# Feed-forward part of a vision layer: eight groups written out, down weights turned behind gate/up, down result scaled in PSUM, last store in two halves

## What is computed

```python
def _act_fake_quant(x, clip_factor):
    scale = jax.nn.sigmoid(clip_factor) * jnp.max(jnp.abs(x)) / QMAX
    return jnp.clip(_ste_round(x / scale), -QMAX - 1.0, QMAX) * scale
xq = _act_fake_quant(x, clip_x[0])          # x = layernorm(h)
gate = jnp.einsum('bsh,ih->bsi', xq, _weight_fake_quant(w_gate))
up = jnp.einsum('bsh,ih->bsi', xq, _weight_fake_quant(w_up))
h = _act_fake_quant(jax.nn.silu(gate) * up, clip_down[0])
return jnp.einsum('bsi,hi->bsh', h, _weight_fake_quant(w_down))
```

## Time and profile before

| | |
|---|---|
| median of 3 runs | 777.65 us (776.64 to 777.92) |
| profiled execution, its own time | 776.94 us |
| its span, first to last instruction | 775.1 us |
| busy share: PE, DVE, ACT, POOL | 89%, 83%, 75%, 68% |
| mean granted TensorE clock | 0.966 |
| feed-forward part within the span | 675.1 to 775.1 us |

### The profile page before, as it was taken

How to read it: one execution, slowest core, us unless ns; L and a number is a source line. 1 busy time by engine, 2 the same in 40 slices (tenths; PEclk the granted TensorE clock), 3 DMA queues, 4 the chain that set the end, 5 groups by cost and what they waited for, 6 DMA issues and landing times. The chain is left out here.

```text
span 775.1 us, 26199 instructions
## 1 busy us (share of the span) xinstructions
PE 686.7 (89%) x9862; PEld 536.8 (69%) x9862; DVE 645.5 (83%) x1396; ACT 582.4 (75%) x1278; POOL 523.8 (68%) x791
## 2 busy tenths in 40 slices
PE   0498899999999999999999999999999999378674
PEld 0277678777877777878877877788788777244363
DVE  4788876899889988989898889889886997769957
ACT  3567878778788678869777877788778886379593
POOL 3449965957686859877677888388848886521174
PEclk9979999999999999999999999999999999879878
DMA  8301000000010000101000000000000000000014
GB/s 236 100 29 33 17 18 4 32 18 19 1 34 22 15 3 32 34 2 33 18 18 3 18 18 12 25 24 32 19 3 22 20 21 21 1 1 0 1 40 129
DMA packets 14958, 21.91 MB, mean 28 GB/s; under 512 B 1972, under 2 KB 11446, under 8 KB 14840
## 3 DMA queue, kind: packets, MB, share of 16 engines
...
q10 hardware_dynamic: 436, 0.40, 0.2%
...
## 5 line engine op out<-in xcount | busy, mean ns | idle before, releaser
L904 POOL TENSOR_TENSOR k_bd<-kT,rmask 128x400 f32<-128x400 f32 x192 | 167.7, 901 | 7.4 <-PE ps_s L1357 4.3
L805 ACT COPY pT<-ps_w 25x400 f32<-25x400 f32 x192 | 94.6, 493 | 9.3 <-PE ps_w L1372 6.7
L1398 PE MATMUL ps_w<-oy_hi,o_hi 128*128 128x512 f32 x192 | 94.9, 494 | 0.0
L913 POOL TENSOR_TENSOR prob_hi<-prob_hi,rsum 128x800 f32<-128x800 f32 x48 | 74.8, 1558 | 13.4 <-DVE rsum L1150 13.3
L1133 DVE TENSOR_REDUCE nmax<-ps_s 128x16 f32<-128x400 f32 x96 | 72.4, 766 | 11.5 <-PE ps_s L1357 11.3
L785 ACT COPY v_bd<-ps_w 50x256 f32<-50x256 f32 x192 | 70.3, 366 | 13.3 <-PE ps_w L1332 10.9
L1398 PE MATMUL ps_w<-oy_hi,o_lo 128*128 128x512 f32 x192 | 76.3, 397 | 0.0
L1398 PE MATMUL ps_w<-oy_lo,o_hi 128*128 128x512 f32 x192 | 76.2, 397 | 0.0
L826 ACT ACTIVATE ps_w<-ps_w 128x256 f32<-128x256 f32 x96 | 35.7, 372 | 51.8 <-PE ps_w L1398 50.4
L918 POOL TENSOR_TENSOR ln<-ln,ln_eps 128x1 f32<-128x1 f32 x96 | 20.0, 208 | 75.2 <-ACT ps_w L826 74.8
L1357 PE MATMUL ps_s<-k_bd,qT 64*25 64x200 f32 (+1 forms) x3072 | 70.5, 291 | 0.0
...
## 6 DMA issues: line engine op xcount, KB each, us to landing
...
```

The source lines that it names most:

```text
L805: last = nc.scalar.copy(pT[ROWB * h:ROWB * h + LQ, s % 2, c::2, :, 0:LQ], ps_w[row:row + LQ, bank].rearrange("p (j t) -> p j t", j=4)[:, : ...
L904: last = nc.gpsimd.tensor_tensor(k_bd[:, v % KBD, c], kT[:, w % 2, c, 2 * p * L:(2 * p + 2) * L].unsqueeze(1).broadcast_to([P, HR, 2 * L]) ...
L913: nc.gpsimd.tensor_tensor(pr, pr, rsum[:, s % 2, e].unsqueeze(2).broadcast_to([P, H, WIDTH[e]]), ALU.mult).then_inc(prob_ready, 1)
L1398: mm = nc.tensor.matmul(G[:], ot[:, s % 2, c, 2 * (p % 2):2 * (p % 2) + 2].rearrange("p b t -> p (b t)"), wt[:, w, c], start=False, stop=( ...
```

## The change

1. All hardware loops of the feed-forward part become straight-line code with constant addresses.
2. Head: the shift is made from `-mean*rstd`, computed while PE turns the maximum, so that scale and shift come out of one instruction. Two memsets move from DVE to POOL. POOL casts only two pairs of group 0, DVE casts the other two. The cast of the down weights comes behind the casts of groups 0 and 1 on POOL.
3. The down weights are turned at the end of gate/up, into banks 3 and 0 of `ps_w`, and ACT copies them out in place of DVE.
4. Down: the product with step and `drow` is written back to the PSUM banks it was read from; the addition reads `hidden` and PSUM; `o_s` is gone. PE waits for `result_ready` (the addition) in place of `down_read`.
5. Group 7 is scaled, added and stored in two halves of two pairs; the first waits for the sixth of the last twelve matmuls (`half_filled`).

```diff
     id32 = sb(stack, "id32", [P, P])
     id16 = sb(stack, "id16", [P, P], BF16)
     stat3 = sb(stack, "stat3", [P, NPAIR, 4])
-    rstd3 = sb(stack, "rstd3", [P, NPAIR])
+    norm3 = sb(stack, "norm3", [P, 2, NPAIR])
+    rstd3 = norm3[:, 0]
...
-    o_s = sb(ffn, "o_s", [P, 2, PAIRS, D])
...
-            with sp.Fori(0, GROUPS) as g:
-                sp.wait_ge(result_ready, g + 1 + T)
+            pieces = [(g * PAIRS, PAIRS) for g in range(GROUPS - 1)] + [(NPAIR - PAIRS, PAIRS // 2), (NPAIR - PAIRS // 2, PAIRS // 2)]
+            for i, (n, pairs) in enumerate(pieces):
+                sp.wait_ge(result_ready, i + 1 + T)
                 for row, b in HALVES:
-                    sp.dma_start(out[bass.ds(g * GB, GB)].rearrange("(q two) t d -> two t q d", two=2)[b],
-                                 hidden[row:row + L, bass.ds(g * PAIRS, PAIRS), :]).then_inc(stored, 16)
-            sp.wait_ge(stored, 32 * GROUPS)
+                    sp.dma_start(out[2 * n:2 * (n + pairs)].rearrange("(q two) t d -> two t q d", two=2)[b],
...
@@ -1522,8 +1527,12 @@
                     if f == 3 and g < GROUPS - 1:
                         y_out(1, GROUPS - 1)
 
+            for k, bank in enumerate((3, 0)):
+                act.wait_ge(wd_turned, k + 1)
+                nc.scalar.copy(wdT[:, :, k * P:(k + 1) * P],
+                               ps_w[:, bank].bitcast(BF16)[:, 0:FC * P].rearrange("p (f t) -> p f t", f=FC)).then_inc(wd_ready, 1)
             act.wait_ge(hstep_chain, 4)
...
             pool.sem_inc(hq_ready, 2 * T)
             pool.sem_inc(yq_ready, T)
+            nc.gpsimd.memset(mx[:], 0.0).then_inc(f_zeroed, 1)
+            nc.gpsimd.memset(one_f[:], 1.0).then_inc(f_zeroed, 1)
             nc.gpsimd.memset(w_q[:, :, I:], 0.0).then_inc(f_zeroed, 1)
+
+            def y_cast(g, pairs=PAIRS):
+                pool.wait_ge(yint_ready, g + 1)
+                if g > 0:
+                    pool.wait_ge(yint3_ready, g + 1)
+                pool.wait_ge(yT_filled, g - 1 + T)
+                nc.gpsimd.tensor_copy(y_q[:, g % 2, :, 0:pairs].rearrange("p k q t -> p q k t"),
+                                      y_int[:, g % 2, 0:pairs].rearrange("p q (k t) -> p q k t", k=KC)).then_inc(yq_ready, 1)
+            y_cast(0, PAIRS // 2)
+            y_cast(1)
             pool.wait_ge(wint_ready, KC)
             nc.gpsimd.tensor_copy(w_q[:, :, 0:I], w_int[:]).then_inc(wq_ready, 1)
-            for g in range(GROUPS):
-                pool.wait_ge(yint_ready, g + 1)
-                pool.wait_ge(yint3_ready, g + 1)
-                pool.wait_ge(yT_filled, g - 1 + T)
-                nc.gpsimd.tensor_copy(y_q[:, g % 2].rearrange("p k q t -> p q k t"),
-                                      y_int[:, g % 2].rearrange("p q (k t) -> p q k t", k=KC)).then_inc(yq_ready, 1)
+            for g in range(2, GROUPS):
+                y_cast(g)
             nc.gpsimd.memset(h_q[:, :, :, :, L:], 0.0).then_inc(f_zeroed, 1)
             for g in range(GROUPS):
                 r = g % 2
...
             for row, _ in HALVES:
                 nc.vector.tensor_reduce(mx[row:row + L, 0:1], tok[row:row + L, 0], AX.X, ALU.max).then_inc(y_max, 1)
+            dve.sem_inc(acts_ready, T)
+            dve.sem_inc(result_ready, T)
+            nc.vector.scalar_tensor_tensor(norm3[:, 1], mean, -1.0, rstd, ALU.mult, ALU.mult).then_inc(dev_chain, 1)
             dve.wait_ge(max_turned, 1)
...
             dve.wait_ge(step_chain, 1)
             nc.vector.reciprocal(mx[:, 4:5], sg[:, 0, 0:1]).then_inc(step_chain, 1)
             dve.wait_ge(step_chain, 2)
-            nc.vector.tensor_scalar(tok[:, 2], rstd, mx[:, 4:5], None, ALU.mult).then_inc(y_ready, 1)
-            dve.wait_ge(y_ready, 1)
-            nc.vector.scalar_tensor_tensor(tok[:, 3], mean, -1.0, tok[:, 2], ALU.mult, ALU.mult).then_inc(y_ready, 1)
+            dve.wait_ge(dev_chain, 4)
+            nc.vector.tensor_scalar(tok[:, 2:4], norm3[:], mx[:, 4:5], None, ALU.mult).then_inc(y_ready, 1)
...
                 largest(g, FP - 1, g * FP + FP)
-            dve.wait_ge(y_ready, 2)
+            dve.wait_ge(y_ready, 1)
             y_ints3(0, 0, 2)
+            dve.wait_ge(yint3_ready, 1)
+            nc.vector.tensor_copy(y_q[:, 0, :, PAIRS // 2:].rearrange("p k q t -> p q k t"),
+                                  y_int[:, 0, PAIRS // 2:].rearrange("p q (k t) -> p q k t", k=KC)).then_inc(first_q, 1)
             y_ints3(1, 1)
-            for k in range(KC):
-                dve.wait_ge(wd_turned, k + 1)
-                nc.vector.tensor_copy(wdT[:, :, k * P:(k + 1) * P],
-                                      ps_s[:, 1, k].bitcast(BF16)[:, 0:FC * P].rearrange("p (f t) -> p f t", f=FC)).then_inc(wd_ready, 1)
-            with dve.Fori(0, GROUPS // 2 - 1) as g2:
+            for g2 in range(GROUPS // 2 - 1):
...
 
-            def scaled(g, r):
+            def scaled(g, r, first=0, pairs=PAIRS):
+                ps = down_ps(r)[:, first:first + pairs]
+                nc.vector.scalar_tensor_tensor(ps, ps, sg[:, 1, 0:1], drow[:].unsqueeze(1).broadcast_to([P, pairs, D]),
+                                               ALU.mult, ALU.mult).then_inc(down_scaled, 1)
+                dve.wait_ge(down_scaled, g + first // 2 + 1)
+                h = hidden[:, g * PAIRS + first:g * PAIRS + first + pairs, :]
+                nc.vector.tensor_tensor(h, h, ps, ALU.add).then_inc(result_ready, 1)
+            for g in range(GROUPS - 1):
                 dve.wait_ge(down_filled, g + 1 + T)
-                nc.vector.scalar_tensor_tensor(o_s[:, r], down_ps(r), sg[:, 1, 0:1], drow[:].unsqueeze(1).broadcast_to([P, PAIRS, D]),
-                                               ALU.mult, ALU.mult).then_inc(down_read, 1)
-                dve.wait_ge(down_read, g + 1 + T)
-                h = hidden[:, bass.ds(g * PAIRS, PAIRS), :]
-                nc.vector.tensor_tensor(h, h, o_s[:, r], ALU.add).then_inc(result_ready, 1)
-            with dve.Fori(0, GROUPS // 2) as g2:
-                for r in (0, 1):
-                    scaled(g2 * 2 + r, r)
+                scaled(g, g % 2)
+            dve.wait_ge(half_filled, 1)
+            scaled(GROUPS - 1, 1, 0, PAIRS // 2)
+            dve.wait_ge(down_filled, GROUPS + T)
+            scaled(GROUPS - 1, 1, PAIRS // 2, PAIRS // 2)
 
...
                 pe.wait_ge(yq_ready, g + 1 + T)
+                if g == 0:
+                    pe.wait_ge(first_q, 1)
                 need(pe, yT_ready, g)
                 for k in range(KC):
...
-                    if isinstance(g, int) or r == 0:
-                        pe.wait_ge(wd_ready, KC)
                 for k in range(KC):
...
                     mm.then_inc(up_filled, 1)
             find_max(0)
             pe.wait_ge(drow_filled, 2)
-            pe.wait_ge(wq_ready, 1)
-            pe.wait_ge(f_zeroed, 3)
-            for k in range(KC):
+
+            def turn_wd(k, bank):
+                pe.wait_ge(wq_ready, 1)
+                pe.wait_ge(f_zeroed, 3)
                 for f in range(FC):
-                    mm = nc.tensor.transpose(ps_s[:, 1, k].bitcast(BF16)[:, f * P:(f + 1) * P], w_q[:, k, f * P:(f + 1) * P], id16[:])
+                    mm = nc.tensor.transpose(ps_w[:, bank].bitcast(BF16)[:, f * P:(f + 1) * P], w_q[:, k, f * P:(f + 1) * P], id16[:])
                 mm.then_inc(wd_turned, 1)
...
+            pe.wait_ge(silu_ready, GROUPS * FC - 2 + 3)
+            turn_wd(1, 0)
             find_max(1)
-            with pe.Fori(0, GROUPS // 2) as g2:
+            pe.wait_ge(wd_ready, KC)
+            for g2 in range(GROUPS // 2):
                 for r in (0, 1):
                     g = g2 * 2 + r
-                    pe.wait_ge(down_read, g - 1 + T)
+                    pe.wait_ge(result_ready, g - 1 + T)
                     for a in (0, 1):
                         pe.wait_ge(hq_ready, 2 * g + a + 1 + 2 * T)
                         for p in range(PAIRS):
                             for f in range(FP * a, FP * a + FP):
                                 mm = nc.tensor.matmul(down_ps(r)[:, p], h_q[:, r, f, 2 * p:2 * p + 2].rearrange("p b t -> p (b t)"),
                                                       wdT[:, f], start=(f == 0), stop=(f == FC - 1), skip_group_check=True)
+                            if g == GROUPS - 1 and a == 1 and p == PAIRS // 2 - 1:
+                                mm.then_inc(half_filled, 1)
                     mm.then_inc(down_filled, 1)
     ffn.close()
     stack.close()
```

30 lines of the change are left out of this document (16 added, 14 removed).

## The result

| | before | after |
|---|---|---|
| median of the runs | 776.94 us (774.22 to 779.27, 9 runs) | 772.93 us (9 runs); 772.40 us (769.84 to 776.04) without one disturbed run |
| ratio, with its 95% interval | | 0.9946 (0.9921 to 0.997) |
| profiled execution: own time, span | 776.94, 775.1 | 769.84, 768.1 |
| attention part within the span | 675.5 | 674.7 |
| feed-forward part | 99.6 | 93.4 |

The profiled execution is the fastest of the rest: its 7.1 us are more than the medians' 4.0 (4.5 without the disturbed run).

What follows compares the result with a forecast made beforehand. DVE was taken to bound gate/up and down, an instruction chain the head, a store the end. Terms -1.5, -0.2, -2.8 and -1.3 sum to -5.8 us: 771.1 from the profiled execution, 771.8 from the median; forecast 771.5, range 770.1 to 772.7.

Steps and rivals of the forecast that it cites:

- Gate/up: Gate/up stage: DVE sets its time, so the stage keeps its length and only starts earlier.
- Head: Start of the feed-forward part: a shorter chain of single instructions up to the first products, -1.5 us.
- Rival A: Head: the DVE and POOL casts of group 0 get in each other's way; 772.0 us, chance 0.2.
- Down weights later: End of gate/up: PE's transposes and ACT's copies fit into idle time, 0 us.
- Second scale: Before `h_int`: the loop's branch and register instructions between DVE's scale and ACT go, -0.2 us.
- Down: Down part: additions reading PSUM run undisturbed by POOL at 1.21 us, ACT becomes the bound, -2.8 us.
- Rival B: Down part: the addition stays at 1.90 us beside POOL's casts; 774.5 us, chance 0.08.
- C: Down part: DVE reads and writes the same PSUM banks at half rate; slower, 778.4 us, chance 0.04.
- Last store: End of the kernel: earlier issue and only 200 KB stored last, -1.3 us.
- Rival D: Head: it gives nothing because another wait takes its place; 773.0 us, chance 0.08.
- rival E: Feed-forward part: straight-line code stalls the instruction queues; 774 to 778 us, chance 0.05.

Runs made afterwards that it cites:

- wq_first: The changed kernel with POOL's cast of the down weights ahead of the y casts again; 777.43 us (one run).
- after_again: The changed kernel once more, unaltered; 772.19 us (12 runs), ratio 0.9943 to the kernel before.
- psum_only: The kernel before with only the down result scaled in its PSUM banks and PE waiting for the addition; 773.81 us, ratio 0.9958.
- head_only: The kernel before with only the changed head and the later turning of the down weights; 775.48 us, ratio 0.9974.
- no_halves: The changed kernel with group 7 scaled, added and stored in one piece; 774.34 us (one run).
- sbuf_again: The changed kernel with the scaled down result in SBUF (`o_s`) again, PE waiting for the scaling only; 774.38 us (one run).
- unrolled_only: The kernel before with only the feed-forward part's loops written out; 774.84 us, ratio 0.9981.
- layout_kept: store48 plus unused PE matmuls ahead of the down part, six `h_int` moved to DVE, and the SBUF places of before; 768.51 us, ratio 0.9915.
- store48: The changed kernel with each store of 50 rows cut into one of 48 rows and one of 2; 771.08 us, ratio 0.9937.

## Why the prediction was right, and where not

**Gate/up, DVE the bound, nothing gained inside:** right. From the second product to the first instruction of the second scale are 43.82 us before and after.

**Head, -1.5:** right, -1.65 at the first gate matmul. The wait for POOL is shown by wq_first. Rival A did not happen: POOL's cast of 512 elements took 0.65 where 0.62 was estimated. But DVE's took 0.43 where I had 0.68, so the two overlapped for 0.18 us only and not for 0.5, too short to tell whether one waits for the other. What I did not have is 0.46 more by the second product. The table parts it. From the first gate matmul to the second product are 6.40 or 6.41 us in the three kernels with loops, 6.12 or 6.13 in eight of those without, 5.88 to 5.95 in three. So 0.28 is the loops' again, at their first turn: "the written-out loop gives DVE nothing" holds for the stage but not for its start. The other 0.18 is the clock. PE's pairs of matmuls fall from 0.87 to 0.50 us when the clock reaches its 2.4 GHz level, and in the changed kernel's two profiles that is not at the same matmul. First after_again (first gate matmul at 679.83), then after (681.66):

```profile
682.47 0.87 PE L1702 MATMUL ps_w<-yT,wgT 128*128 128x400 bf16 x2
683.13 0.88 PE L1707 MATMUL ps_s<-yT,wgT 128*128 128x400 bf16 x2
684.46 0.50 PE L1702 MATMUL ps_w<-yT,wgT 128*128 128x400 bf16 x2
```

```profile
684.30 0.70 PE L1702 MATMUL ps_w<-yT,wgT 128*128 128x400 bf16 x2
684.83 0.50 PE L1707 MATMUL ps_s<-yT,wgT 128*128 128x400 bf16 x2
```

I had taken PE "at the same speed", and 0.2 us is what that leaves to chance.

**Down weights later, 0:** right. ACT still waits 4.25 us for DVE's scale.

**Second scale, -0.2:** right, -0.26, in every kernel without loops and in none with them. The chain ahead of ACT, from DVE's first instruction to its scale, is not the same to a tenth: 2.5 us before, 2.4 after, 2.2 in seven other profiles, with loops or without.

**Down, -2.8:** the mechanism is right in each piece, the size holds for this one profile. From the first `h_int` to the last addition 33.27 became 30.08, -3.2; psum_only has -2.7 of it. I read the 33.27 from an execution in which PE's first group took 5.30 us, took it for the kernel's own time, and said only that this group falls off the path. With a first group of 4.15 us the old down part needs 31.80 (head_only), and the gain is some 1.5 less. That the profile and the one behind it had the same late first group (5.30 and 5.28) is chance. The addition is 1.22, the casts 1.19, ACT the pace at 25.03 for 48. Rival B falls with the additions of 1.22 beside POOL's casts, and C with the product of 1.29 from PSUM to PSUM. The 62 cycles more for a PSUM source that the Trainium skill gives (VectorE: DVE Perf Modes, The TRN2 errata), by estimate 0.065 us, do not show: 1.22 with one input in PSUM, 1.22 and 1.23 with both in SBUF and POOL still.

**Last store, -1.3:** the mis-sized term, -0.5 in the profile. Halving gives 0.7 in all (no_halves), of which 0.46 in the tail. I had seen that group 6's store and the first half would be ahead of the last data, and sized this queue too short: group 6's data from 0.4 us behind its addition, and some 4.9 us for the two groups. In the trace its first data start 0.84 us behind its addition, 1.94 ahead of the end of the last one, and the 819,200 bytes of groups 6 and 7 take 5.1 us (161 GB/s), until 3.15 behind it. With the 0.7 that follow, that is the tail. The quicker down part is not needed for this: after_again has a pause in the data before group 6's store, and sbuf_again stores the groups before it at the old pace of 3.26 us; their tails are 3.89 and 3.97. The other 50-row profile with halves, wq_first, moved the same bytes in 4.7 us and has 3.45, for which no run shows a cause. Stores of 48 rows take 0.4 off in the mean of five profiles.

**Sum.** In the two profiles the feed-forward part lost 6.2 us, -5.8 was forecast. That they agree so well is partly luck: the last store gave 0.8 less than its term, and the stretch up to the second product (0.46), the chain of the second scale (0.1), the head (0.15) and the down part (0.4 over its term) gave it back. Rival D and, for this part, rival E fall with it.

**Yet the medians differ by 4.0 and 4.9 us, not 6.2.** The measured 772.93 us is 1.4 over the forecast of 771.5 and inside its range. What the medians lack is either in the attention part, whose instructions are the same, or in the draw of 99.6 us for the part of before. I take the attention part as a run's own time less the profile's feed-forward part, less 1.8 us (own time over span: 1.84 and 1.74), which counts every run of before with that 99.6. Means: before 675.7 us (78 runs, standard error 0.2), psum_only and unrolled_only 675.1 (24 runs, 0.4), the ten kernels with `norm3` in the place of `rstd3` 677.2 (50 runs, 0.3), layout_kept 676.6 (6 runs, 0.9). Nothing in my sum had a term for a part that is not changed; I wrote that up to 675 us nothing changes. Three causes are left. First, the 675.7 of before may be too low: if its runs had on the mean an earlier first down group than the profile, their feed-forward part was up to 1.5 us shorter and the attention part as much longer, 677.2 at the most, which would be the whole difference. Only the profile shows the parts, so no run tells how often that was so. The same holds for unrolled_only. Of the old places psum_only alone is free of this, 675.7 (12 runs, 0.6). Second, the new pair moves every tensor behind it by 128 bytes: for that speak 50 runs at 677.2 and psum_only. Third, it is the luck of the executions: for that speaks layout_kept, whose mean is no better. Six runs that scatter by 5 us can't tell 1.5, and no further kernel was tried.

What PE does in a long attention part can be seen. PE in wq_first, in a row of 128 equal matmuls, with SP loading `x_in`:

```profile
538.68 1.21 PE L1383 MATMUL ps_w<-pT,v_bd 128*32 128x50 f32 x89
539.37 1.90 SPq L628 DMA_DIRECT2D x_in<-in_w_gate  x2
542.15 0.70 PE L1383 MATMUL ps_w<-pT,v_bd 128*32 128x50 f32 x39 [2.27 <-issue]
```

and in its windows:

```profile
540.00:542.00 2.00, 0.00 (x0) 0.00 (x0) 1.47 (x4) 0.16 (x1) 1.95 (x2) 1.00 0.47 141
542.00:544.00 2.00, 1.85 (x45) 1.73 (x45) 0.52 (x2) 1.10 (x3) 1.92 (x5) 0.65 0.24 64
544.00:546.00 2.00, 2.00 (x12) 1.81 (x10) 1.92 (x6) 0.59 (x1) 1.04 (x2) 0.50 0.00 0
```

PE stands for 2.27 us after 89 of them, waiting for nothing that the profile shows, and comes back at the 1.2 GHz level. psum_only does the same row without the stop:

```profile
537.74 1.62 PE L1382 MATMUL ps_w<-pT,v_bd 128*32 128x50 f32 x128
```

Stops of this kind stand at two places of the program. At about 540 us, always with 39 matmuls of this row left, they last 1.71 to 2.27 us in seven profiles, 0.44 in two (that of before is one) and nothing in five. All seven are of the ten profiles with `norm3` in the place of `rstd3`, none of the four with the old places, which speaks for the places without proving them. At about 560 us, with 31 matmuls left, they last 0.75 to 1.11 in nine profiles, 0.49 in head_only, 1.70 in store48 and nothing in three. Those of 0.75 us or more sum to 1.11 us or less in six profiles (attention part 674.6 in the mean, 672.9 to 675.5) and to 1.7 or more in eight (678.3 in the mean, 676.4 to 681.5).

The traces point at what PE waits for. The DMA queue that the profile calls instruction, q8, moves packets of 16,384 bytes. The one at the stop in wq_first (540 us) started at 539.93 and took 0.94; the DMA view of 539.90 to 540.90 us has one packet there:

```profile
q8 instruction: 1, 0.02, 5.9%
```

It ended at 540.87, 0.99 after PE had reached the place of the stop (539.89), and PE went on 1.28 us after that end. In all 20 stops at the two places, of 0.44 to 2.27 us, PE goes on 1.22 to 1.44 us after the end of such a packet. In the eight cases without a stop the packet had ended 2.1 to 6.6 us before PE came to the place. In psum_only, for one, it ended at 532.32, and PE came at 538.95. The Trainium skill (Runtime: NRT & Kernel Launch, Instruction fetch mechanics) has the sequencer fetch its code in blocks of 16 KiB through a DMA queue of its own while it executes, the cost "mostly hidden". The trace agrees with the blocks, and here the cost is hidden only when a block starts early enough. No experiment moved a block by itself, so this rests on the 28 timings. The load of `x_in` does not hold the block up by its data: they begin 0.5 to 1.0 us after the start of the block in all seven long stops. What makes the block start late, and whether the places of the tensors have a part in it, no run shows.
